# Attention: the products of probabilities and values of two slots issued back to back

## The reference

```python
attn = jnp.einsum('bhqd,bhkd->bhqk', q, k) / jnp.sqrt(jnp.asarray(hd, x.dtype))
alibi = -slopes[None, :, None, None] * (Tt - 1 - jnp.arange(Tt, dtype=x.dtype))[None, None, None, :]
attn = attn + alibi
causal = jnp.tril(jnp.ones((Tt, Tt), dtype=bool))[None, None, :, :]
attn = jnp.where(causal, attn, jnp.finfo(x.dtype).min)
p = jax.nn.softmax(attn, axis=-1)
out = jnp.einsum('bhqk,bhkd->bqhd', p, v).reshape(Bb, Tt, C)
return out @ Wo + bo
```

## Time and profile before

| | |
|---|---|
| median of 3 runs | 1429.78 us (1424.3 to 1432.53) |
| span of the profiled execution | 1444.0 us |
| granted TensorE clock, mean | 0.858 |
| TensorE busy (matmuls) | 1081.1 us, 75% |
| VectorE busy | 790.8 us, 55% |
| ScalarE busy | 517.8 us, 36% |
| GpSimd busy | 501.2 us, 35% |

### The profile page before, as it was taken

One profiled execution on the slowest core, in us unless ns is written; L12 is line 12 of the kernel. 1 busy time (PEld: TensorE's weight loads), 2 busy tenths in 40 slices (PEclk: granted clock), 3 DMA queues, 4 the chain that ended last, 5 costly groups with the idle time before them and its releaser, 6 DMA issues. The chain is left out here.

```text
span 1444.0 us, 20692 instructions
## 1 busy us (share of the span) xinstructions
PE 1081.1 (75%) x6895; PEld 632.7 (44%) x6896; DVE 790.8 (55%) x2091; ACT 517.8 (36%) x814; POOL 501.2 (35%) x538
## 2 busy tenths in 40 slices
PE   5762149903898999999999989887476877676676
PEld 4651136702244444444454444433244766565443
DVE  4757810044867787878778887761252333333326
ACT  1330013403066556655566545554211221111113
POOL 3110064055016101520154103342444256665633
PEclk9975568955589999999999989987699898999898
DMA  4226013323213111311222121013431432222135
GB/s 117 73 63 109 1 39 106 92 43 91 67 28 97 36 37 47 97 36 36 73 80 80 44 68 52 25 38 143 164 102 34 105 86 77 82 80 63 37 107 185
DMA packets 90021, 106.09 MB, mean 73 GB/s; under 512 B 16882, under 2 KB 69883, under 8 KB 87285
## 3 DMA queue, kind: packets, MB, share of 16 engines
q1 hardware_dynamic: 76862, 79.08, 19.1%
q0 software_dynamic: 13072, 25.90, 6.5%
HBM read 63.29 MB, written 37.95 MB: 70 GB/s over the span
## 5 line engine op out<-in xcount | busy, mean ns | idle before, releaser
L2005 DVE TENSOR_REDUCE maxima<-psum 128x1 f32<-128x512 f32 (+4 forms) x624 | 390.7, 644 | 118.7 <-PE psum L1825 60.7
L1939 ACT ACTIVATE probs<-psum 128x1024 f32<-128x1024 f32 (+3 forms) x384 | 300.6, 809 | 306.8 <-PE psum L1840 237.5
L1820 PE MATMUL psum<-ka,qa 75*128 75x512 bf16 (+3 forms) x768 | 245.4, 352 | 42.6 <-DVE maxima L2005 30.3
L1836 PE MATMUL psum<-qa,ka 78*128 78x512 bf16 (+3 forms) x768 | 211.0, 337 | 4.3 <-ACT probs L1939 4.0
L116 POOL DMA_INDIRECT expert_out<-g_y,g_place x160 | 155.2, 970 | 123.2 <-issue 88.1
L1853 PE MATMUL psum<-probs,v_wide 128*32 128x512 f32 (+3 forms) x1536 | 171.5, 520 | 0.0
L1820 PEld LDWEIGHTS psum<-ka,qa 75*128 75x128 bf16 x768 | 69.6, 101 | 188.7 <-DVE maxima L2005 143.6
L1357 POOL DMA_INDIRECT got<-expert_out,to_row x64 | 66.4, 1038 | 188.0 <-ACT probs L1939 128.4
L2475 DVE TENSOR_TENSOR g_y<-psum,g_gate 128x512 f32<-128x512 f32 x40 | 27.7, 692 | 154.4 <-DMA expert_out<-g_y,g_place 139.3
L1836 PEld LDWEIGHTS psum<-qa,ka 78*128 78x128 bf16 x768 | 75.5, 101 | 79.0 <-ACT probs L1939 28.7
L1840 PE MATMUL psum<-mask_k,ident_b 128*128 128x128 bf16 x512 | 107.1, 228 | 0.0
(11 more groups left out here) (325 smaller groups left out, 1653.2 us busy)
## 6 DMA issues: line engine op xcount, KB each, us to landing
g_rows<-sorted SPq DMA_DIRECT2D x160, 65.0 KB
qa<-q_steps SPq DMA_DIRECT2D x45, 192.0 KB
ka<-k_steps SPq DMA_DIRECT2D x15, 576.0 KB
f_got<-expert_out SPq DMA_DIRECT2D x16, 512.0 KB, 11.1
w<-in_W SPq DMA_DIRECT2D x16, 256.0 KB
w_gu<-in_gu SPq DMA_DIRECT2D x1, 4096.0 KB, 18.6
q_steps<-q_parts SPq DMA_DIRECT2D x12, 256.0 KB
k_steps<-k_parts SPq DMA_DIRECT2D x12, 256.0 KB
```

The costliest lines, as they stand in the source:

```text
L1820: mm = pe.matmul(bank[:, h * width:(h + 1) * width], qa[b][0:ROWS_MAX, h0 + h, qt * P:(qt + 1) * P], ka[b][0:ROWS_MAX, h0 + h, seg * HALF: ...
L1836: mm = pe.matmul(out, ka[s.buf][0:ROWS_ALL, h, j * P:(j + 1) * P], qa[s.buf][0:ROWS_ALL, h, q0:(c + 1) * HALF], start=True, stop=True, ski ...
L1939: act.activation(probs[k % PRING][:, 2 * pair:2 * pair + 2, 0:w], PS[:, 2 * pair:2 * pair + 2, 0:w], ACT.Exp).then_inc(exps, 1)
L2005: dve.tensor_reduce(maxima[:, seg, h0:h0 + heads, qt], bank[:, 0:heads * width].rearrange("p (h k) -> p h k", h=heads), AX.X, ALU.max).the ...
```

## The change

In an odd slot no product is issued any more. In an even slot k from 2 on, the products of slots k - 2 and k - 1 are issued one behind the other; in slot 0 of a step those of slots 10 and 11 of the step before, and after the last step both at its end. The ring of probabilities has four tiles instead of three. What is computed, and in which order the products are summed, stays the same.

```diff
-PRING = 3
+PRING = 4
...
-                        if k:
+                        if k and k % 2 == 0:
+                            emit_pv(s, k - 2)
                             emit_pv(s, k - 1)
-                        elif not flags[0]:
+                        elif k == 0 and not flags[0]:
                             before = Step(s.n - 1, (s.buf - 1) % BUFS, 0)
+                            emit_pv(before, SLOTS - 2)
                             emit_pv(before, SLOTS - 1)
...
                 last = Step(STEPS - 1, (STEPS - 1) % BUFS, 0)
+                emit_pv(last, SLOTS - 2)
                 emit_pv(last, SLOTS - 1)
```

## The result

| | before | after |
|---|---|---|
| median | 1427.75 us (4 runs, 1424.3 to 1432.53) | 1483.60 us (4 runs, 1479.51 to 1490.79) |
| ratio, 95% interval | | 1.0393 (1.0348 to 1.0438) |
| profiled execution | span 1444.0 us | 1483.8 us, span 1482.1 us |
| attention: first exponential to last product | 599.6 us | 653.4 us |

The change costs 56 us. The direction was forecast, the size was not: 1458 us were predicted with 1438 to 1474 as the range, and the measurement lies above it, at twice the forecast rise. So the comparison is of the attention: +53.8 us.

What follows compares the result with a forecast made beforehand. TensorE, busy 558 of 594 us in the attention, was expected to wait for VectorE and ScalarE in odd slots. 18.4 + 8.6 + 1.5 gave +28.5 us: 1472.5 profiled, 1458 as median, range 1438 to 1474.

Steps and rivals of the forecast that it cites:

- Sum: Whole attention: twelve steps 18.4 us, three steps with side units 8.6, last step 1.5; in all +28.5 us.
- rival 3: Attention: emptier odd slots add half as much time at TensorE's lower clock, +12 us, 1470; 12 in 100.
- light pair: Two neighbouring slots such as 5 and 6: 0.21 us saved, new waits 0.48, old wait 0.16 gone; net +0.13 us.
- side steps: Steps 0, 4 and 8, with a side unit ending slots 4 to 11: +2.86 us each, 8.6 together.
- step 15: Last step, without units: slots 7 and 8 +0.7 us, slots 9 and 10 likewise, 1.5 us together.
- rival 4: Odd slots shrink nowhere, each pair costs what its moved product adds (0.88 us at 512 columns): +71, 1500; 3 in 100.
- Size of a product and of a pair: Products of 512 columns: one takes 1.00 us, two adjacent 1.88; 0.21 us saved against two apart.
- Rival 1: TensorE is the bound and waits don't grow: -20 us, 1410; 6 in 100.
- The pair walked: Slots 5 and 6 of a plain step: 5.77 us against 5.64 before, with new waits of 0.31 and 0.17.
- Slots 9 and 10: Slot 9 gains nothing, its product lying under VectorE's chain; slot 10 grows by 0.88 us per step with next maxima.
- What costs nothing: Fourth probabilities tile never waits; output copying and later loads wait some 0.5 us longer, at no cost.
- What would show it: Profile after: 16-matmul groups of 1.88 us, plain step 34.3, slot 10 at 4.2, weight-load waits rising from 110 and 29.

Runs made afterwards that it cites:

- warm: Kernel before, with unread matmuls in TensorE's longest waits (slot 10 of steps 1 and 5, slot 9 of steps 7 and 11): 1423.43 us, ratio 0.9954.
- fill9: Changed kernel, with five unread matmuls of 512 columns added in slot 9 of each step with maxima: 1480.35 us, ratio 1.0350 to the kernel before.
- before_again: Kernel before, run again without an edit: 1433.60 us, ratio 1.0009.
- after_again: Changed kernel, run again without an edit: 1484.51 us, ratio 1.0382 to the kernel before.
- ring3: Changed kernel with three tiles of probabilities instead of four: 1486.72 us, ratio 1.0387 to the kernel before.
- fill_more: Changed kernel with unread matmuls in slot 9 and more in slots 10, 9 and 6 of some steps: 1474.02 us, ratio 1.0318 to the kernel before.

## Why the prediction was wrong

**The step that failed is the Sum**, in two of its terms. It put the clock at nothing and gave it to rival 3, with 12 in 100 and +12 us; and it carried the 1.53 us of one plain step to all twelve, and 0.13 to each light pair of the side steps. In their place the runs showed 11 to 13 us for the clock and 12.5 for the dearer pairs, of the +52 to +54 in the attention where +28.5 were forecast. The direction was right, and so was the mechanism of the walk: lost covers, and slot 10 as the dearest place.

*The clock.* The time at the lower level doubled, from 44 to 48 us to 85 to 96. What a microsecond of it costs is measured: 11/27 = 0.41 in warm, 11/34 = 0.33 in fill9. For the 41 to 48 us more that makes 14 to 20. Rival 3 assumed that the low time would grow by half; it doubled. And it had the place in hand. It reckoned that slot 9's product lies under VectorE's chain and that slot 10 becomes the longest piece of TensorE's work, and did not put the two together: the hole comes in the slot ahead of the pair. The Trainium skill (TensorE: Matmul & The Clock Gate, A second HAM failure mode: psum-queue depth-cycling) says that short idles of TensorE between groups of matmuls, from cycling PSUM banks, can make the clock go back and forth. The trace agrees in this much, with 1.32 us of idle ahead of the 0.69; here the idle comes from VectorE's chain, and the same idle in steps 0, 4, 8 and 12 was followed by no fall in slot 10.

*The rest.* Taking for each slot the fastest execution of either kind (before, before_again, warm; after, after_again, ring3, fill9, fill_more), which takes most of the clock out, the attention is 583 and 624 us: +41. Of these, steps 0, 4 and 8 have 12.0 (forecast 8.6), step 15 has 1.5 (1.5) and the twelve others 27.6 (18.4). The 1.53 for a step is exact in step 3 (1.54); the other eleven lie between 1.1 and 3.8, eight of them at 2.0 or more. The price of a light pair was taken from one of them and let stand for all five, and for all steps. In step 6 slot 5 shrinks by 0.78 us but slot 6 grows by 1.64 even at full clock, 0.86 for the pair: the price that rival 4 put on a pair (0.88), though not by its way, since the odd slot does shrink. There ScalarE's extra jobs (the row at 642.44) are the reason that the trace shows. That VectorE's small operations and such jobs also make the other dear places is likely and not shown. So of the +53.8 and +52.1 of the two couples of profiles 28.5 were forecast, 12.5 are mis-sized pairs (41 - 28.5), and 11 to 13 are left for the clock, a little under the 14 to 20 above. The border between the last two is an estimate: some low time is left in either minimum, and the choice of the fastest of five executions against the fastest of three favours the kernel after a little.

Point by point:

- **Size of a product and of a pair**: right. 1.86 us (1.88 predicted), and the saving of 0.21 showed as 0.20 once the readers were fast. The Trainium skill (TensorEngine Tiling (Array Packing), Key Properties) has the change of mode as what drains TensorE; the 0.20 agrees. Rival 1, which is that rule alone, was wrong, since the earlier trace rows hold a covered reading under each product.
- **The pair walked**: right, 5.75 for 5.77. (The parts given beside it, 0.48 less 0.21 and 0.16, add up to 0.11 and not to the 0.13 between the two ends; the sum used 0.13.) Its two waits exist: with VectorE's shortened, ScalarE's alone holds the pair at +0.28.
- **Slots 9 and 10**: right at full clock. Slot 9 changed by 0.00, slot 10 by 0.86 (predicted 0.88) in after_again; 2.20 in the first profile, with the clock.
- **Side steps**: slots 5 and 6, 7 and 8, 9 and 10 of step 4 cost 0.73, 0.82 and 0.86 (0.75, 0.84, 0.88). The other three pairs cost 0.22, 0.46 and 0.26 for the 0.13 each that were carried over. Step 4 takes 42.2 us where some 42 were predicted: 3.3 more than before instead of 2.86.
- **Step 15**: slots 7 and 8 take 5.21 us, 4.47 before, +0.74 for the predicted 0.7.
- **What costs nothing**: right for the ring. The copying of the outputs does stand longer: ScalarE waits for the last product ahead of it ten times, 7.6 us in all and at most 2.2, where it waited four times, 2.5 us in all. The prediction had some 0.5 us later in each step and nothing lost by it; whether any of the 5 us reached TensorE no run shows.
- **What would show it**: the plain step (34.4 us in after_again for 34.3), slots 9 and 10, the products' groups of 16 matmuls and the idle time ahead of L1820 and L1836 (42.6 to 54.3 and 4.3 to 8.7 us on the pages) came out as said. The waits of weight loads did not. Those for maxima were to rise from 110 us; they fell to 88.8. Those for probabilities were to rise from 28.7; they fell to 22.8.

Waits of the kernel after, from 389 to 1037.7 us, beside the earlier trace rows:

```profile
ACT probs L1942 <- PE psum L1840: 212.1, 126, 7.4
...
DVE maxima L2008 <- PE psum L1825: 114.1, 85, 4.4
...
PEld psum L1820 <- DVE maxima L2008: 88.8, 202, 2.6
ACT probs L1942 <- PE psum L1836: 83.0, 54, 5.3
...
PE psum L1812 <- DVE neg_max L2017: 20.6, 15, 1.8
```

A row of the same view of the kernel before, from 402 to 996 us:

```profile
PE psum L1812 <- DVE neg_max L2014: 4.9, 14, 0.5
```
and, in its timeline, the load of weights behind the product of the earlier trace rows that ends at 524.56:

```profile
524.56 0.10 PEld L1820 LDWEIGHTS psum<-ka,qa 75*128 75x128 bf16 x1 [0.84 <-DVE maxima L2005]
```

Half of the 110 us was never standing. Behind a single product the load of the next unit's weights shows 0.84 us of idle "for maxima", though TensorE is busy with the product all this time; such loads, 80 of them, hold 54 of the 110 us. Behind a pair the same 0.84 is put down to "issue" (the row at 524.49 above), and loads behind products hold 1.2 of the 88.8. Idle of weight loads under a running matmul is no idle of TensorE. Among the rows of PE itself L1812 waiting for neg_max rose from 4.9 to 20.6 us, which is slot 9's hole. VectorE and ScalarE also wait longer for TensorE: 56.2 to 114.1 us for the masked units and 178.0 to 212.1 for the masked scores.

## What to carry to other kernels

A product that covers somebody else's work is not overhead, however many gaps it brings: before work is bunched, look for what runs beneath each piece, and move it only to where a longer chain is bare, as the pair in slot 9. When an edit opens a hole on TensorE, put the hole and the work behind it together: if the busiest piece comes next, it may run at half the clock. And a price walked in one plain step is a price for that step; walk one of each kind before multiplying by twelve.

## What the runs showed of the chip

- Behind a hole of 1.32 us in an otherwise busy step the granted clock went from 1.00 to 0.69. In the first profile after, slot 10 grew in 9 of 16 steps by over 1.3 us (1.68 to 3.14) instead of 0.86; in the second in 8 (1.76 to 2.48). Behind holes of the same length in steps 0, 4, 8 and 12 it grew by 0.86 each time.
- At the lower level a pair of products takes 3.57 us, at the full one 1.86. The attention pays 0.33 to 0.41 us for each microsecond there (fill9, warm), less than the half that it would be if TensorE alone set the pace.
- Matmuls that nobody reads, in holes that exist anyway, made the kernel before 0.5% faster (0.9954, 0.9929 to 0.998), though it already had 0.96.
